# Context attention of a gated layer: each quad's softmax sums replicated over its rows, inverted on ScalarE and multiplied on VectorE

## The reference, cut to what matters

```python
q = jnp.einsum('bsc,hcd->bhsd', xn, wq)          # 512 queries
k = jnp.einsum('btc,hcd->bhtd', yn, wk)          # 77 context keys
v = jnp.einsum('btc,hcd->bhtd', yn, wv)
a = jax.nn.softmax(jnp.einsum('bhsd,bhtd->bhst', q, k) * D ** (-0.5), axis=-1)
o = jnp.einsum('bhst,bhtd->bhsd', a, v)
o = o.transpose(0, 2, 1, 3).reshape(x.shape[0], x.shape[1], H * D)
x_out = x + o @ li1_w + li1_b
```

## Time and profile before

| | us |
|---|---|
| three runs, median (lowest, highest) | 1772.88 (1769.68, 1773.03) |
| the profiled execution, its own time | 1774.03 |
| its span | 1772.3 |
| mean granted TensorE clock | 0.921 |
| busy in the span: TensorE / VectorE / ScalarE / GpSimd | 1523.8 / 870.2 / 744.5 / 148.9 |

### The profile page before, as it was taken

One profiled execution on the slowest core, in us unless ns is written; L12 is line 12 of the kernel. 1 busy time (PEld: TensorE's weight loads), 2 busy tenths in 40 slices (PEclk: granted clock), 3 DMA queues, 4 the chain that ended last, 5 costly groups with the idle time before them and its releaser, 6 DMA issues.

```text
span 1772.3 us, 21984 instructions
## 1 busy us (share of the span) xinstructions
PE 1523.8 (86%) x8796; PEld 686.8 (39%) x8814; DVE 870.2 (49%) x1674; ACT 744.5 (42%) x1313; POOL 148.9 (8%) x209
## 2 busy tenths in 40 slices
PE   5748999889899989988479999898999889888296
PEld 2223333342344436623133333423444347433284
DVE  4464776443556453334645884524664541446212
ACT  2553556323445325243544555243454153252043
POOL 0000111100012000000000112000021000011331
PEclk9968999999899989998779999999899989999598
DMA  4000000000000100000000000000000100030241
GB/s 196 1 1 0 1 1 1 0 1 1 0 1 1 48 1 0 1 1 2 1 1 1 1 1 1 0 1 1 1 1 6 43 0 1 1 83 1 81 137 61
DMA packets 18105, 30.27 MB, mean 17 GB/s; under 512 B 4640, under 2 KB 12640, under 8 KB 17104
## 3 DMA queue, kind: packets, MB, share of 16 engines
q1 hardware_dynamic: 16752, 26.23, 4.6%
q0 software_dynamic: 1248, 2.59, 0.4%
HBM read 23.62 MB, written 5.19 MB: 16 GB/s over the span
## 4 chain that ended last, share of the span: by engine, by line
PE 78%; DVE 9%; ACT 8%; issue 2%; DMA 1%; POOL 1%; SPq 0%; POOLq 0%; DVEq 0%; ACTq 0%
PE ps L837 7%; PE ps L944 5%; PE ps L711 4%; PE ps L883 4%; PE ps L651 3%; PE ps L1399 3%; PE ps L1411 3%; PE ps L1075 3%; PE ps L750 3%; PE ps L1083 2%; PE ps L995 2%; PE ps L896 2%; PE ps L975 2%; PE ps L688 2%; PE ps L684 2%
## 5 line engine op out<-in xcount | busy, mean ns | idle before, releaser
L2102 DVE TENSOR_REDUCE peak<-ps 128x1 f32<-128x512 f32 x256 | 163.1, 682 | 97.4 <-PE ps L837 97.4
L1714 ACT ACTIVATE big<-ps 128x512 f32<-128x512 f32 x256 | 138.5, 596 | 114.1 <-PE ps L875 113.9
L837 PE MATMUL ps<-pp,qT 32*128 32x512 f32 x512 | 148.7, 668 | 1.4 <-ACT pp L1837 1.4
L866 PE MATMUL ps<-qT,pp 32*128 32x512 f32 x512 | 148.2, 653 | 0.0
L1737 ACT ACTIVATE big<-ps 128x512 f32<-128x512 f32 (+3 forms) x256 | 101.1, 436 | 101.4 <-PE ps L975 100.4
L2147 DVE TENSOR_REDUCE crest<-ps 128x2 f32<-128x512 f32 (+3 forms) x128 | 105.2, 824 | 66.4 <-PE ps L950 66.3
L975 PE MATMUL ps<-qT,pp 32*128 32x128 f32 (+3 forms) x512 | 123.1, 479 | 0.0
L1653 ACT ACTIVATE big<-ps 77x1024 f32<-77x1024 f32 x96 | 93.2, 1017 | 65.8 <-PE ps L711 65.8
L2043 DVE TENSOR_REDUCE small<-ps 128x8 f32<-128x616 f32 x96 | 76.8, 800 | 80.7 <-PE ps L684 46.4
L944 PE MATMUL ps<-pp,qT 32*128 32x384 f32 (+3 forms) x512 | 110.5, 502 | 5.0 <-DVE crest L2147 3.0
L1633 ACT ACTIVATE sq<-ps 128x512 f32<-128x512 f32 x48 | 28.7, 597 | 192.7 <-PE ps L651 192.7
(11 more groups left out here) (492 smaller groups left out, 2686.0 us busy)
## 6 DMA issues: line engine op xcount, KB each, us to landing
big<-in_w SPq DMA_DIRECT2D x23, 256.0 KB, 3.3
pt<-in_l2w SPq DMA_DIRECT2D x2, 2048.0 KB, 7.6
w_l<-in_l SPq DMA_DIRECT2D x1, 3086.0 KB, 18.2
pp<-in_w SPq DMA_DIRECT2D x1, 2048.0 KB, 9.9
big<-by_expert SPq DMA_DIRECT2D x23, 66.0 KB, 2.0
by_expert<-cst SPq DMA_DIRECT2D x1, 1472.0 KB, 16.6
cst<-in_const SPq DMA_DIRECT2D x1, 1427.5 KB, 7.1
w_l<-in_l SPq DMA_DIRECT2D x1, 1218.0 KB, 9.2
```

The lines of the kernel that those rows point to most:

```text
L837: pe.matmul(rbank(x), qT[at, u, k, 128 * i:128 * i + 128], keyT(u, k)[at, :], start=True, stop=True, tile_position=(32 * c, 0)).then_inc(* ...
L866: pe.matmul(a1_bank(y), keyT(u, k)[at, 128 * j:128 * j + 128], qT[at, u, k, :], start=True, stop=False, tile_position=(32 * c, 0))
L1714: A(prob(m)[:, TURN_OF[g], :], a1_bank(tplace(m, g)), ACT.Exp).then_inc(*SCALAR.did("a1", "exp", m, g))
L2102: v.tensor_reduce(peak[:, p // 4 % 2, i, c:c + 1], rbank(ring(p, c)), AX.X, ALU.max)\
```

## The change

Sums: the stationary operand is now a block of ones, so that each head's sum stands in all its 32 rows at once, and each quad's sums are a group of their own in PSB[1], overwritten by the next quad's. Before sums(u, k), TensorE waits for the Ln of the quad before.

Inverting: ScalarE takes Ln of PSB[1] into a buffer of its own for each quad (four of them in rs and sq, used in slot 0 and again in slot 1) and Exp with scale -1 in place. The copies of PSB[0] and PSB[1] and VectorE's reciprocal are gone.

Dividing: VectorE multiplies PSB[0] by that buffer straight into qT[:, u, k, :]. values of the next quad waits for this product. In VectorE's order the products of slot 0's quads 0 to 2 stand between the maxima of slot 1, ahead of `cut_off(1)`; the rest follow it.

Spreading is gone. li1 of slot 0 goes between values(1, 2) and sums(1, 3), into PSB[4], and li1 of slot 1 behind values(1, 3), into PSB[5], each product behind a wait for its quad.

On ScalarE the inverse of quad k - 1 follows the exponentials of quad k, and the inverse of quad 3 those of quad 3.

```diff
+        def inverses(u, k):
+            return (rs if k % 4 < 2 else sq)[:, k % 2, :]
...
                     pe.wait_ge(*SCALAR[tag, "exp", u, 2 * k + 1])
-                    if u and k == 0:
-                        pe.wait_ge(*SCALAR[tag, "den", 0])
+                    if u or k:
+                        pe.wait_ge(*SCALAR[tag, "log", u if k else 0, (k - 1) % 4])
                     for c in range(4):
-                        mm = pe.matmul(PSB[1][32 * c:32 * c + 32, :],
-                                       K["col8"][0:KC, 128 * k + 32 * c:128 * k + 32 * c + 32], cprob(u, k)[:, c, :],
-                                       start=k == 0, stop=k == 3, tile_position=(0, 32 * c), skip_group_check=True)
+                        mm = pe.matmul(PSB[1][32 * c:32 * c + 32, :], K["ones"][0:KC, 0:32], cprob(u, k)[:, c, :],
+                                       start=True, stop=True, tile_position=(0, 32 * c), skip_group_check=True)
...
                     elif u or k:
-                        pe.wait_ge(*SCALAR[tag, "o", u if k else 0, (k - 1) % 4])
+                        pe.wait_ge(*VECTOR[tag, "O", u if k else 0, (k - 1) % 4])
...
+                def li1(u):
+                    if u == 0:
+                        pe.wait_ge(*SCALAR[tag, "exp", 1, 5])
+                    for c in range(4):
+                        pe.wait_ge(*VECTOR[tag, "O", u, c])
+                        mm = pe.matmul(PSB[4 + u], W["l1"]["a2_li1"][:, 128 * c:128 * c + 128], qT[:, u, c, :], start=c == 0,
+                                       stop=c == 3)
+                    mm.then_inc(*TENSOR.did("a2 li1", u))
...
                 if dh == 8:
                     shares(0)
+                else:
+                    li1(0)
                 sums(1, 3)
                 values(1, 3)
                 if dh == 8:
                     shares(1)
-                    return
-                for u in U:
-                    pe.wait_ge(*VECTOR[tag, "inv", u])
-                    for k in range(4):
-                        at = 4 * u + k
-                        if at >= 6:
-                            pe.wait_ge(*VECTOR[tag, "O", 0, at - 6])
-                        for c in range(4):
-                            row = 32 * c + 8 * k
-                            mm = pe.matmul(PSB[2 + at % 6][32 * c:32 * c + 32, :],
-                                           K["ident"][:, row:row + 1].to_broadcast([128, 32]), rs[:, u, :], start=True,
-                                           stop=True, tile_position=(0, 32 * c))
-                        mm.then_inc(*TENSOR.did(tag, "spread", u, k))
+                else:
+                    li1(1)
...
-                reduce4("a2 li1", w["a2_li1"], lambda u: qT[:, u, :, :],
-                        lambda u: [SCALAR["a2", "o", 1, 3], VECTOR["a2", "O", u, 3]])
...
+                def inverted(u, k):
+                    act.wait_ge(*TENSOR[tag, "den", u, k])
+                    if u:
+                        act.wait_ge(*VECTOR[tag, "O", 0, k])
+                    A(inverses(u, k), PSB[1], ACT.Ln).then_inc(*SCALAR.did(tag, "log", u, k))
+                    act.wait_ge(*SCALAR.last())
+                    A(inverses(u, k), inverses(u, k), ACT.Exp, scale=-1.0).then_inc(*SCALAR.did(tag, "inv", u, k))
...
+                if dh == 32:
+                    for u in U:
+                        for a in range(8):
+                            exp(u, a)
+                            if a >= 3 and a % 2:
+                                inverted(u, a // 2 - 1)
+                        inverted(u, 3)
+                        if u == 0:
+                            shifted(1)
+                    return
...
+                def over(u, k):
+                    v.wait_ge(*TENSOR[tag, "AV", u, k])
+                    v.wait_ge(*SCALAR[tag, "inv", u, k])
+                    v.tensor_tensor(qT[:, u, k, :], PSB[0], inverses(u, k), ALU.mult).then_inc(*VECTOR.did(tag, "O", u, k))
...
                         maxima(u, a)
+                        if dh == 32 and u and a % 2 and a > 1:
+                            over(0, a // 2 - 1)
                     cut_off(u)
...
-                    v.scalar_tensor_tensor(x2[:, u, :], lin(u), w["a2_li1_b"], x1[:, u, :], ALU.add, ALU.add)\
+                    v.scalar_tensor_tensor(x2[:, u, :], PSB[4 + u], w["a2_li1_b"], x1[:, u, :], ALU.add, ALU.add)\
```

More of the change, by code:

```diff
@@ L1656, in out @@
                 def out(u, k):
-                    act.wait_ge(*TENSOR[tag, "AV", u, k])
                     if dh == 8:
+                        act.wait_ge(*TENSOR[tag, "AV", u, k])
                         if k % 2:
@@ L1687, in cross @@
                         out(1, (a - 5) // 2)
[L1688 to L1695, removed]
+                share(0)
                 out(1, 3)
+                inverse(0)
+                share(1)
+                inverse(1)
             def attend():
@@ L2052, in cut_off @@
                         .then_inc(*VECTOR.did(tag, "cut", u))
-                def inverse(u):
-                    v.wait_ge(*SCALAR[tag, "den", u])
-                    v.reciprocal(rs[:, u, :], sq[:, u, :]).then_inc(*VECTOR.did(tag, "inv", u))
+                def over(u, k):
+                    v.wait_ge(*TENSOR[tag, "AV", u, k])
+                    v.wait_ge(*SCALAR[tag, "inv", u, k])
+                    v.tensor_tensor(qT[:, u, k, :], PSB[0], inverses(u, k), ALU.mult).then_inc(*VECTOR.did(tag, "O", u, k))
                 def joined(u, hf):
@@ L2085, in cross @@
                     return
[L2086 to L2093, removed]
+                over(0, 3)
+                for k in range(4):
+                    over(1, k)
             def attend(residual_of):
```

## The result

| | before | after |
|---|---|---|
| median of four runs each, us | 1771.37 | 1755.54 |
| lowest, highest | 1769.68, 1773.03 | 1748.86, 1756.37 |
| profiled execution: own time, span | 1774.03, 1772.3 | 1756.37, 1754.6 |
| mean granted clock | 0.921 | 0.919 |

The ratio is 0.9902 (95% interval 0.9875 to 0.993). The kernel is faster by 16 us where 28 were forecast, and 1.5 us above the range.

What follows compares the result with a forecast made beforehand. TensorE, 78% of the chain, was taken to bound the kernel. Savings of 13.2 us in turn 1 and 15.2 in turn 2, 28.4 together, took 1774.03 to 1745.6, and 1744.5 us as a median; range 1740 to 1754.

Steps and rivals of the forecast that it cites:

- C: ScalarE switches tables between Ln and Exp, 1.28 us a reload; 7 us a turn lost, gain 14, 1759 us; chance 0.04.
- Product (0,2): VectorE's product for slot 0's quad 2 ends near 403.05 us, so values(0,3) starts at about 403.15 instead of 402.68.
- The second turning: Turning of slot 1's maxima, turned(1), goes at 404.1 us instead of 403.60, a loss of 0.5 us.
- B: ScalarE, with 0.15 us a quad in hand, paces slot 1: gain 19 to 26, 1747 to 1754 us; chance 0.12.
- Later stages at other phases of the clock: up to 3 us either way, the spread of the three runs: Outside the edited stage: an unknown price of up to 3 us either way, from runs at 1769.68 to 1773.03.
- The sign that the prediction set for turn 2: Behind the stage in turn 2: the norm's first matmul at about 1185.15 us, 1198.35 less turn 1's 13.2.
- the give-back in the next MLP: MLP behind the stage: the gain given back there would show the prediction wrong; no size given.
- the sum takes 2.4 GHz throughout: Edited stage, both turns: clock stays full since the two 1.50 us gaps ahead of its fall are gone; gain 28.4 us.
- 9 us of which it priced as low clock taken out: Edited stage: price if the clock falls as before, 3.5 us in turn 1 and 5.5 in turn 2.
- the clock rows of before left as they are: Edited stage with the clock falling as in the old profile: gain 19.4 us instead of 28.4.
- Rival A: The clock falls in the new stage too: price 9 us, gain 19.4, 1753.5 us; chance 0.18.

Runs made afterwards that it cites:

- four fillers: Changed kernel with 4 unread matmuls on TensorE ahead of the norm behind the stage, both turns: 1745.33 us (0.9861), again 1746.51 us (0.9858).
- six and twelve: Changed kernel with 6 or 12 unread matmuls ahead of the norm behind the stage, both turns: 1748.67 us (0.9874) and 1749.50 us (0.9888).
- eight and sixteen: Changed kernel with 8 or 16 unread matmuls ahead of the norm behind the stage, both turns: 1755.19 us (0.9916) and 1762.49 us (0.9950).
- the stalls filled: Kernel before with 7 unread matmuls in each of the two 1.50 us waits of values (1,1) and (1,2): 1769.65 us, ratio 0.9965.

## Why the prediction was wrong

**The stage: right, step by step.** Ln of slot-wide tiles out of PSUM took 594 ns and Exp 630 (0.597 and 0.626 in the earlier trace rows), the product 692; there were no table loads between them, so C is out. Product (0,2) ended at 402.57 us, 403.05 forecast, in a trace that runs 0.5 us ahead from its start. The second turning came 0.6 us late (0.5 forecast). Slot 1 ran without a stall, so B is out. li1 took 3.63 us a slot (3.53), norm at 425.73 (426.0). Turns 12.9 and 15.0 us, 27.9 against 28.4.

**The failed step: "Later stages at other phases of the clock: up to 3 us either way, the spread of the three runs".** In place of 3 us, 10.3 were lost outside the stages. The sign that the prediction set for turn 2, the norm's first matmul at 1185.15 us, was missed by 8.6 us, which is just what the lead fell by between the stages (13.5 to 4.9); the give-back in the next MLP, which it named as a sign of being wrong, was 1.7 us of that. The term was sized by three runs of one kernel. That was too few (seventeen spread over 12.4 us), and such runs keep the places of their stages, which the change moves by 13 us. Shifts by fillers alone moved the changed kernel by 12 us (1743.6 to 1755.6 less the fillers; 11 by the ratios) and the kernel before by 6 (1772.4 to 1778.1). That the lost time goes with the low clock is shown by the traces. That most of it is a matter of place and not of the changed code is shown by four fillers, which give back 6 us or more, twice; six and twelve support it within their noise, eight and sixteen don't.

**With it fell the sentence that "the sum takes 2.4 GHz throughout".** It booked the whole shortening of the stage as time off the end, 9 us of which it priced as low clock taken out. The stage did run at full clock, but the total of low stretches stayed: 280.1 and 283.1 us. The 19.4 us that the prediction gave for "the clock rows of before left as they are" is near what span times clock shows, 19.8, within the rounding of the clock. Rival A had that sum and 1753.5 us, close to the medians, but that is luck: the falls came behind the stage and ahead of the next, not in it. The 9 us themselves were nearly right; with the stalls filled the two stages gave 6.8, and 1.8 of the missing 2.2 are the wait for the reciprocal and the fillers' own time.

The Trainium skill's rule (TensorE: Matmul & The Clock Gate, Part 1), that activity releases the throttle and idleness brings it back, was read for the stage alone. The runs agree with it: filling one idle stretch kept off the fall behind it. But the kernel before passed the same idle stretch, 3.03 us ahead of 445.99, at 1.00, so that an idle stretch alone does not say whether the clock falls. The prediction did not ask what the next ones would do.

**What stays open.** Averaged over the six places tried, less the fillers, the changed kernel stands at 1749.4 us (the two medians of four fillers taken as 1744.2), the kernel before over five at 1774.3: 24.9 us apart, against 17.8 between the unshifted ones; by the ratios 24.5, against 18.9. So some 6 to 7 of the 10 us are the places of these two kernels, an estimate from few places with intervals of some 3 us each. The other 3 or 4 may belong to the change, through the norm's idle stretch behind the stage, which is low in both turns of the changed kernel, or be the unevenness of so few places. Why one place is better than another, and why one execution of a kernel has its falls elsewhere than the next, was not worked out.

## What to carry to other kernels

Price a change in its own stage by the chain, and allow for the clock outside it separately: from runs with shifts of a few matmuls, several runs of each, not from the spread of three runs of one kernel. Where idle stretches of some 3 us are spread over a kernel, look at span times mean granted clock beside the time; it stayed within 3.5 us over nine runs of one kernel that differed by 7.5. It is no measure of what was gained: with the spreading cut short it fell by 9 us and the time didn't. Taking out one block of a serial tail (here 8.7 us of spreading) can give 0.2 us when another engine's work was hidden under it; take out the whole tail.

## What the hardware showed that was not expected

The clock's loss is large and mobile: up to 140 of 1772 us by span times clock. In the changed kernel it fell behind an idle stretch of 3 us at 429.5 us, which the kernel before had passed at 1.00 some 13 us later in its own time. Four bf16 matmuls of 0.215 us at one place moved the median of the whole kernel by -8 to -9 us in one version (-6 by the ratios) and by +7 in the other. And executions of one and the same kernel can differ by 12 to 15 us with the clock that they get: 1764.19 to 1776.63 in the kernel before, 1741.92 to 1757.01 with li1 not moved, 1760.97 to 1776.13 with the stalls filled.
